# Gated cross-attention block on one core: the first LayerNorm only centres, and its deviation scales the exponential

## The reference

```python
# x: (2, 1024, 256), ctx_1024: (2, 77, 256), 8 heads of 64
x = x + tanh(g_xattn[0]) * xattn(layernorm(x), ctx_1024, Wq, Wk, Wv, Wo, bo)
x = x + tanh(g_ffn[0]) * ffn(layernorm(x), w1, b1, w2, b2)
# layernorm: (x - mean) / sqrt(var + 1e-5)
# xattn: softmax((x Wq)(ctx Wk)^T / 8) (ctx Wv) per head, then @ Wo + bo
# ffn: linear 256 -> 1024, relu, linear 1024 -> 256; inputs, hidden values
#      and weights rounded to fixed point of 8 bits
```

## Time and profile before

| | |
|---|---|
| median of 3 runs (lowest to highest) | 129.49 us (129.15 to 129.62) |
| the profiled execution | 129.84 us, of which the span of its instructions is 127.9 us |
| busy share PE, PEld, DVE, ACT, POOL | 95%, 86%, 78%, 56%, 73% |
| chain that ended last, by engine | PE 55%, POOL 27%, issue 7%, DVE 5% |
| starts of PE's slots 0 to 9, us | 21.86, 27.79, 33.62, 38.55, 46.95, 52.20, 57.87, 63.94, 69.97, 76.38 |

### The profile page before, as it was taken

How to read it: one execution, slowest core, us unless ns; L and a number is a source line. 1 busy time by engine, 2 the same in 40 slices (tenths; PEclk the granted TensorE clock), 3 DMA queues, 4 the chain that set the end, 5 groups by cost and what they waited for, 6 DMA issues and landing times.

```text
span 127.9 us, 2834 instructions
## 1 busy us (share of the span) xinstructions
PE 121.3 (95%) x996; PEld 110.4 (86%) x996; DVE 99.8 (78%) x221; ACT 71.3 (56%) x151; POOL 93.7 (73%) x175
## 2 busy tenths in 40 slices
PE   7999999999995999999999999999999999999990
PEld 2698978989893799999999899999999999888780
DVE  6109888599999879999897969697887979547882
ACT  4124625599793828499392829282837546365520
POOL 3002873777979898989998998988768596987720
PEclk9999999999999999999999999999999999999999
DMA  3898898100000000000002000200020020001014
GB/s 113 244 297 300 292 399 350 68 3 5 3 3 0 0 0 8 0 0 0 5 0 82 0 0 5 82 0 3 5 82 0 0 85 5 0 29 58 24 58 164
DMA packets 5572, 8.86 MB, mean 69 GB/s; under 512 B 1180, under 2 KB 2743, under 8 KB 5431
## 3 DMA queue, kind: packets, MB, share of 16 engines
q1 hardware_dynamic: 5559, 8.69, 19.2%
HBM read 6.59 MB, written 2.10 MB: 68 GB/s over the span
## 4 chain that ended last, share of the span: by engine, by line
PE 55%; POOL 27%; issue 7%; DVE 5%; DMA 2%; ACT 2%; POOLq 0%; DVEq 0%
PE of_ps L776 12%; PE sc_ps L743 11%; PE h_ps L803 7%; PE of_ps L818 6%; PE tr_ps L692 5%; PE tr_ps L755 4%; POOL rstd L286 4%; POOL yq L290 4%; POOL x_sb L343 3%; POOL probs L277 3%; POOL hid L322 3%; POOL xn L272 3%; DMA ctx_sb<-in_ctx_dram 2%; POOL rstd L266 2%; PE h_ps L712 1%
## 5 line engine op out<-in xcount | busy, mean ns | idle before, releaser
L776 PE MATMUL of_ps<-u_sb,pT 128*128 128x256 f32 x240 | 31.5, 282 | 0.3
L743 PE MATMUL sc_ps<-a_sb,xT 128*128 128x308 f32 x192 | 31.2, 311 | 0.0
L776 PEld LDWEIGHTS of_ps<-u_sb,pT 128*128 128x128 f32 x240 | 29.9, 188 | 1.0 <-issue 0.7
L743 PEld LDWEIGHTS sc_ps<-a_sb,xT 128*128 128x128 f32 x192 | 27.5, 189 | 0.8 <-issue 0.6
L422 ACT ACTIVATE hid_q<-h_ps,b1z 128x256 int8<-128x256 f32 x58 | 24.9, 495 | 3.9 <-PE h_ps L803 3.9
L396 ACT ACTIVATE probs<-probs 128x616 f32<-128x616 f32 x16 | 11.6, 722 | 27.7 <-DVE probs L547 27.7
L277 POOL TENSOR_TENSOR probs<-probs,rden 128x616 f32<-128x616 f32 x16 | 19.6, 1224 | 3.7 <-DVE rden L557 3.7
L542 DVE TENSOR_REDUCE mx<-sc_ps 128x8 f32<-128x616 f32 x16 | 12.7, 792 | 7.4 <-PE sc_ps L743 7.4
L322 POOL CAST hid<-hid_q 128x512 bf16<-128x512 int8 x27 | 15.9, 613 | 2.0 <-ACT hid_q L422 2.0
L803 PE MATMUL h_ps<-x2T,w1T 128*128 128x256 bf16 x128 | 16.6, 273 | 0.0
L408 ACT CAST pT<-tr_ps 128x640 fp32r<-128x640 f32 x16 | 11.0, 690 | 7.1 <-PE tr_ps L755 6.8
(11 more groups left out here) (105 smaller groups left out, 184.7 us busy)
## 6 DMA issues: line engine op xcount, KB each, us to landing
w_sb<-in_L_ffn_w_dram SPq DMA_DIRECT2D x2, 1024.0 KB, 11.3
out_dram<-x_sb SPq DMA_DIRECT2D x7, 256.0 KB, 2.5
x_sb<-in_x_dram SPq DMA_DIRECT2D x4, 256.0 KB, 8.2
x_sb<-in_x_dram SPq DMA_DIRECT2D x1, 1024.0 KB, 11.5
wk_sb<-in_L_xattn_Wk_dram SPq DMA_DIRECT2D x2, 256.0 KB, 3.7
wq_sb<-in_L_xattn_Wq_dram SPq DMA_DIRECT2D x1, 512.0 KB, 5.9
wv_sb<-in_L_xattn_Wv_dram SPq DMA_DIRECT2D x1, 512.0 KB, 7.7
wo_sb<-in_L_xattn_Wo_dram SPq DMA_DIRECT2D x1, 512.0 KB, 7.7
```

Of the source, the lines that this page charges most:

```text
L743: ins = nc.tensor.matmul(sc_ps[:, a, 0:HALF], xT[:, T % 2, p, c, :], a_sb[:, q, T // TB, c, HALF * a:HALF * a + HALF], start=first, stop=last)
L776: ins = nc.tensor.matmul(attn_ps, pT[:, T % 2, p, P * c:P * c + P], u_sb[:, q, MC * (T // TB) + c, :], start=first, stop=last)
```

## The change

The rows that go into the scores are now only centred, and with the sign turned: xn = mean - x. The sign and the softmax's 1/8 go into A (`wqT` is copied with the scale -1/8), and the missing division by the deviation becomes the scale of the exponential, one number per row (`rstd1`). The centring of tiles 2 to 15 is an activation on ScalarE (`minus_centred`, L378 after), that of tiles 0 and 1 is on VectorE (L627 after). GpSimd keeps only the reciprocal deviation, always for two tiles. VectorE's statistics come as one tile a slot in slots 1 to 10. In the prologue the context comes as two loads, one from ScalarE, and there is one more warm-up matmul; TensorE's transposes of tiles 0 and 1 stand ahead of the values' projection and the first scores between its two halves; the copy of `vz` for the second pair moves from VectorE to ScalarE.

```diff
-WARM = 6
+WARM = 7
-FIRST_OF = (0, 2, 4, 6, 8, 12)
+FIRST_OF = tuple(range(0, TILES, 2))
...
         def _(sp):
-            sp.dma_start(ctx_sb[:, :, :], ctx_in.rearrange("b m d -> m b d")).then_inc(ctx_in_sb, 16)
+            sp.dma_start(ctx_sb[:, 0, :], ctx_in[0, :, :]).then_inc(ctx_in_sb, 16)
...
-                nc.gpsimd.tensor_scalar(nm1[:, t], mv1[:, t, 0], -1.0, 1.0, ALU.mult, ALU.mult).then_inc(ve1_ready, 1)
-            def normalise_first(T):
-                pool.wait_ge(rstd1_ready, T + 1)
-                if T >= 2:
-                    pool.wait_ge(xT_psum, T - 1)
-                nc.gpsimd.tensor_scalar(xn[:, T % 2, :], x_sb[:, T, :], nm1[:, T:T + 1], rstd1[:, T:T + 1],
-                                        ALU.add, ALU.mult).then_inc(xn_ready, 1)
...
             for s in range(TILES):
-                if s == 2:
-                    rstd_first(6, 8)
-                if s == 4:
-                    rstd_first(8, 12)
-                if live(s + 4) and s > 0:
-                    normalise_first(s + 4)
                 if live(s - 1):
                     normalise_second(s - 1)
                 if live(s + 1):
                     softmax_scale(s + 1)
                 if s in (0, 1):
                     a_low(s, s + 1)
+                if s % 2 == 1 and 3 <= s < TILES - 4:
+                    rstd_first(s + 3, s + 5)
...
-                if s == 6:
-                    rstd_first(12, 16)
...
+            def minus_centred(T):
+                act.wait_ge(mv1_ready, T + 1)
+                act.wait_ge(xT_psum, T - 1)
+                nc.scalar.activation(xn[:, T % 2, :], x_sb[:, T, :], ACT.Identity, bias=mv1[:, T, 0:1],
+                                     scale=-1.0).then_inc(xn_ready, 1)
+
             def exponentials(T):
+                act.wait_ge(rstd1_ready, T + 1)
                 act.wait_ge(centered, T + 1)
-                nc.scalar.activation(probs_v(T), probs_v(T), ACT.Exp, scale=SCALE).then_inc(exp_done, 1)
+                nc.scalar.activation(probs_v(T), probs_v(T), ACT.Exp, scale=rstd1[:, T:T + 1]).then_inc(exp_done, 1)
...
+            act.dma_start(ctx_sb[:, 1, :], ctx_in[1, :, :]).then_inc(ctx_in_sb, 16)
             act.wait_ge(ctxT_psum, 1)
...
-                nc.scalar.copy(wqT[:, 2 * j:2 * j + 2, :].rearrange("p c n -> p (c n)"), h_ps[:, j, :]).then_inc(wqT_ready, 1)
+                nc.scalar.activation(wqT[:, 2 * j:2 * j + 2, :].rearrange("p c n -> p (c n)"), h_ps[:, j, :], ACT.Copy,
+                                     scale=-SCALE).then_inc(wqT_ready, 1)
...
                 if live(s + 3):
                     xT_copy(s + 3)
+                if live(s + 4) and s > 0:
+                    minus_centred(s + 4)
...
             stats_first(0, 2)
-            stats_first(2, 4)
+            for T in range(2):
+                dve.wait_ge(mv1_ready, T + 1)
+                nc.vector.tensor_scalar(xn[:, T, :], x_sb[:, T, :], mv1[:, T, 0:1], -1.0, ALU.subtract,
+                                        ALU.mult).then_inc(xn_first, 1)
...
-                if 1 <= s <= 5:
-                    stats_first(4 + 2 * s, 6 + 2 * s)
+                if 1 <= s and live(s + 5):
+                    stats_first(s + 5, s + 6)
                 if live(s + 2):
                     center(s + 2)
...
-            pe.wait_ge(ctx_in_sb, 16)
+            pe.wait_ge(ctx_in_sb, 32)
```

More of the change, by code:

```diff
@@ L263, in rstd_first @@
                 nc.gpsimd.tensor_scalar(ve1[:, t], mv1[:, t, 1], EPS, 1.0, ALU.add, ALU.mult).then_inc(ve1_ready, 1)
-                nc.gpsimd.tensor_scalar(nm1[:, t], mv1[:, t, 0], -1.0, 1.0, ALU.mult, ALU.mult).then_inc(ve1_ready, 1)
-                pool.wait_ge(ve1_ready, 2 * len([T for T in FIRST_OF if T <= first]))
+                pool.wait_ge(ve1_ready, len([T for T in FIRST_OF if T <= first]))
                 nc.gpsimd.tensor_tensor(rstd1[:, t], ve1[:, t], mhalf[:, 0:end - first], ALU.pow).then_inc(rstd1_ready, end - first)
-            def normalise_first(T):
-                pool.wait_ge(rstd1_ready, T + 1)
-                if T >= 2:
-                    pool.wait_ge(xT_psum, T - 1)
-                nc.gpsimd.tensor_scalar(xn[:, T % 2, :], x_sb[:, T, :], nm1[:, T:T + 1], rstd1[:, T:T + 1],
-                                        ALU.add, ALU.mult).then_inc(xn_ready, 1)
             def softmax_scale(T):
@@ L468, in _ @@
                 nc.scalar.copy(head_blocks(vz, 0, q), pair_bank(0, q)).then_inc(v01_ready, 1)
+            minus_centred(2)
+            minus_centred(3)
+            act.wait_ge(v_psum, 2)
+            for q in range(2):
+                nc.scalar.copy(head_blocks(vz, 1, q), pair_bank(0, q)).then_inc(v23_ready, 1)
             xT_copy(2)
+            exponentials(0)
             u_copy(0, 0)
-            exponentials(0)
             u_copy(0, 1)
             u_copy(0, 2)
+            minus_centred(4)
             act.wait_ge(g_in, 32)
@@ L635, in _ @@
                                     ALU.subtract).then_inc(xT_ready, 2)
-            dve.wait_ge(v_psum, 2)
-            dve.wait_ge(vz_zero, 1)
-            for q in range(2):
-                nc.vector.tensor_copy(head_blocks(vz, 1, q), pair_bank(1, q)).then_inc(v23_ready, 1)
+            stats_first(2, 4)
             center(0)
+            stats_first(4, 6)
             rowsT_low(2)
+            denominators(0)
             u_low(0, 0)
-            denominators(0)
             u_low(0, 1)
@@ L710, in output_weights @@
                     c, row = g // (P // WIN), WIN * (g % (P // WIN))
+                    if (b, j, col) == (0, 2, 0):
+                        pe.wait_ge(v23_ready, 2)
                     dst = u_banks[b, c // 2][:, D * (c % 2):D * (c % 2) + D]
@@ L737, in scores @@
                 for p, q in PARTS:
+                    if q == 1 and T == 0:
+                        pe.wait_ge(a_ready, 2)
                     if p == 1:
@@ L861, in _ @@
             pe.wait_ge(ctxT_ready, 1)
-            keysT(wk_sb, k_psum, (0, 1))
+            keysT(wk_sb, k_psum, (0, 1), 0)
             pe.wait_ge(wk_in[1], 16)
-            keysT(wk_sb, k_psum, (2, 3))
+            keysT(wk_sb, k_psum, (2, 3), 1)
             pe.wait_ge(wq_in, 16)
@@ L882, in _ @@
                 ins.then_inc(xT_psum, 1)
-            keysT(wv_sb, v_psum, (2, 3))
-            pe.wait_ge(a_ready, 2)
+            pe.wait_ge(wv_in, 16)
+            keysT(wv_sb, v_psum, (0, 1), 0)
+            pe.wait_ge(a_high, 2)
+            pe.wait_ge(a_ready, 1)
             scores(0)
-            pe.wait_ge(v23_ready, 2)
+            pe.wait_ge(v01_ready, 2)
+            keysT(wv_sb, v_psum, (2, 3), 0)
             rowsT(2)
             pe.wait_ge(wo_in, 16)
-            pe.wait_ge(v01_ready, 2)
             output_weights(0)
```

19 lines of the change are left out of this document (5 added, 14 removed).

## The result

| | before | after |
|---|---|---|
| median (lowest to highest), 4 runs each | 129.40 us (129.15 to 129.62) | 125.75 us (125.38 to 126.05) |
| the profiled execution, its span | 129.84, 127.9 us | 126.05, 124.1 us |
| starts of PE's slots 0 to 5, us | 21.86, 27.79, 33.62, 38.55, 46.95, 52.20 | 20.40, 26.41, 32.21, 36.99, 43.81, 49.13 |
| starts of slots 6 to 9 and 12, us | 57.87, 63.94, 69.97, 76.38, 94.54 | 54.75, 60.75, 66.75, 72.75, 90.75 |

The ratio is 0.9715, with an interval of 0.9685 to 0.9744: 2.85% faster. The two rows of slot starts show where.

A forecast was written before the change was run, and what follows sets the result against it. PE bounds the kernel, so only its waits can be regained: 1.59 and 0.32 (GpSimd), 0.33 (VectorE), 2 times 0.06 (cold starts), less 0.05, make 2.3 us. Forecast 127.2 us, own range 126.6 to 127.9, 8 in 10 125.3 to 128.4.

The forecast's parts named there:

- GpSimd's removed work: Slots 3 and 8: with normalisations, pair and mean gone, PE's waits of 1.59 and 0.32 us for GpSimd go.
- VectorE's statistics: Slots 1 and 2: one tile a slot brings the residual earlier and ends PE's wait, 0.33 us (0.25 to 0.50).
- ScalarE's new work: Centring on ScalarE, some 0.5 us a slot, is hidden and costs nothing; without cover in slot 1, 0.5 us once.
- The prologue: Before slot 0: PE has next to no gap, so moving blocks gains nothing; 0.05 us taken as loss.
- TensorE's clock rises earlier: Rival, chance 0.17: longer warm-up raises the clock during the keys; Wq 1.2 us sooner, transposes up to 0.4; 125.6 us.
- Two context loads: Prologue: splitting the context's load saves only issue time and brings it no sooner; costed at nothing, -0.1 to +0.3 us.
- 129.9 us for a context 3 us late: Rival, chance 0.05: the context's second load, started by ScalarE, lands late and delays all that follows on PE.
- The 0.05 for the seventh matmul: Prologue: the seventh warm-up fills PE's 0.22 us wait and may move the context's transposes by 0.0 to 0.2 us.
- Cold starts: Blocks after a wait on PE start cold, 0.77 us in place of 0.71; 2 times 0.06 us gained.
- The sum behind slot 0: GpSimd's 1.59 and 0.32, VectorE's 0.33 and 2 times 0.06 for cold starts; 2.36 us without the prologue's 0.05.

The follow-up runs named there:

- the control: The changed kernel itself, run again without an edit in the set of the halved Wq load: 125.82 us (125.31 to 126.08, 6 runs), ratio 0.9730.

## Why the prediction was right, and where it failed

**GpSimd's removed work: right in sum.** Slot 3 gained 1.58 us and slot 8 0.41; the forecast had 1.65 and 0.38. No wait of PE for GpSimd is left. The margin in slot 3 is 0.33 us, forecast 0.19. Not all of it is GpSimd's, though: with the statistics in pairs slot 3 keeps 1.32 (8.40 to 7.08). And the reason was put too broadly. The prediction counts "16 normalisations of 558 ns" among what goes; eleven of them put back at 480 ns bring back 0.21 us of waiting and 0.1 us in all. Most of the 2.07 us was the pair and the mean in front of the second LayerNorm, and by elimination that is what counted. (By the prediction's own numbers PE arrives at 38.44 and not 38.42, so its margin was 0.21.)

**VectorE's statistics: the mechanism was right, the term mis-sized.** It said 0.33 us (0.25 to 0.50), all of it one wait for the residual; undoing the part costs 0.80. The 0.33 counts one wait of PE. VectorE has hardly a gap in slots 1 to 5, so a pair of tiles is late for more than the residual: in slots 3 and 5 PE loses at the attention's output too. Those 0.27 and 0.11 us were not looked for. VectorE at 5.51 us of 6.00 in slots 6 to 10 (forecast 5.6) did no harm.

**ScalarE's new work: right.** A centring takes 525 ns (forecast 500) and is hidden. Slot 1 has ScalarE at 5.31 of 5.80 us. The exponential never waits for `rstd`. What wasn't in the forecast: its scale per row costs 95 ns an instruction, hidden too, by these groups of the changed kernel (count | busy us, mean ns | idle before):

```profile
L384 ACT ACTIVATE probs<-probs,rstd 128x616 f32<-128x616 f32 x16 | 13.1, 817 | 23.0 <-DVE probs L545 23.0
...
L378 ACT ACTIVATE xn<-x_sb,mv 128x256 f32<-128x256 f32 x14 | 7.2, 525 | 0.5 <-DVE mv L535 0.5
```

**The prologue: this step failed.** It said that "moving its blocks gains nothing" and put the whole at -0.05 us; it was 1.46, so the time is outside the forecast's own range of 126.6 to 127.9 us. The sentence reads one profile, in which PE had no gap between the keys and slot 0, and takes the instant at which the clock rises as given. At a given instant the moved blocks do gain nothing: from the block behind the Wq transposes to slot 0 it takes 10.93 us, and took 10.87. The step that failed is the clock, left at its late instant in the sum. Two things were missed.

First, that instant is not fixed by the program. It can be read where the starts of the single matmuls come closer, to about 0.1 us:

| PE's pause ahead of the context's transposes | the clock rises at, us |
|---|---|
| none over 0.05 us (11 profiles) | 3.5, 3.9, 5.1, 5.5, 5.6, 5.8, 5.8, 6.4, 6.5, 6.7, 6.8 |
| 1.90 us (two warm-ups) | 7.3 |
| 0.20 us (two context loads in the kernel before) | 9.2 |
| 0.22 us (before) | 10.2 |

The 6.7 of after and the 3.9 of the control are the same program. The Trainium skill (TensorE: Matmul & The Clock Gate, What's actually happening) says that the instant differs from run to run, and puts it at 0.5 us to either side. The control bears the first out and differs by more, 2.8 us. Every profile with a pause has a later instant than every one without, though the longest pause has not the latest. So the pause that the seventh matmul fills very likely matters. It doesn't act alone: six warm-ups leave no pause when the context lands by 3.5 us, and then the clock rises early too.

Second, an early clock is worth little in the kernel before, which gives back 1.1 us of it in waits (13.38 against 12.28 us), 0.9 of that at the scores, where VectorE's statistics of tiles 2 and 3 hold up `a_sb`. The changed kernel keeps nearly all of it. Of what the change does there, the prediction looked at TensorE's order and not at the call taken out of VectorE's. By the timelines that call is the larger part; TensorE's moved blocks have no price that a run shows, since the run that moves one makes a third order.

So the rival "TensorE's clock rises earlier" (chance 0.17, 125.6 us) is what came, together with the forecast's 2.3 us, and 125.75 us lies in the wider range, 125.3 to 128.4, because of that rival. Its price was right in both parts, 1.2 and 0.4 us for 1.16 and 0.36. That the changed prologue would keep this gain, where the old one doesn't, it didn't ask: there it was lucky. The argument against it, that the runs of before lie close together, was weak: the rise at 6.4 in place of 10.2 us moves slot 0 of the kernel before by only 0.57 us, so close times don't show a steady instant. What fixes the instant stays open.

**Two context loads: right** by the medians, 129.13 us against 129.19. (The prediction's 129.9 us for a context 3 us late should be 130.2, its 127.2 and 3; nothing hangs on it.) The 0.05 for the seventh matmul was nothing: the context's transposes start at 3.70 us in both profiles. **Cold starts**: the transposes of slot 3 take 0.71 us now, and the 0.06 is inside slot 3's 1.58. **The sum behind slot 0** came out at 2.33 us for 2.3 with the help of a term it doesn't have: the layout gives 0.34. That part of the match is luck. The terms that it has gave about 2.0. Slot 2 gained 0.15 of its 0.33, and slots 0 and 4 lost 0.08 and 0.07.

Not tried: the kernel before with the whole new prologue and nothing else, which would give the 1.1 us alone; the same with only `stats_first(2, 4)` moved; and the changed kernel with TensorE's old order in full. These three would share the 1.1 us out.

## What to carry to other kernels

An order without gaps in one profile says only that it fits that execution's clock; where TensorE's rise differs between executions, cost each order at an early and at a late instant, and look on the other engines for an instruction that waits for a load ahead of what TensorE wants. Keep a block of other work between transposes and the matmuls that read them: without one TensorE waited 0.82 us. Where two engines are both without slack, their terms trade: undo one alone before believing either's size. On GpSimd look at the form of an instruction as well as its size before moving it away.

## What the runs showed of the hardware

- One program's TensorE took the 16 key matmuls in 2.34 and in 3.18 us in two executions; of the other twelve profiles ten have 2.34 to 3.44 us and two 4.36 and 4.44. The clock rose at 3.5 to 6.8 us in the 11 without a pause ahead of the context's transposes and at 7.3 to 10.2 in the 3 with one.
- After a wait of 1.57 us and 1.7 us of work at the full rate TensorE ran at half rate from 10.3 to nearly 14 us in one execution; after a wait of 1.20 us in another it did not.
- GpSimd's operation on 128 x 256 with two operations takes 1145 ns as subtract then multiply by a constant, 480 ns as multiply by a constant then add, and 558 ns as add then multiply with two row operands. VectorE does subtract and multiply in 340 ns.
- A scale that is read per row makes ScalarE's exponential of 128 x 616 take 817 ns, not 722. The Trainium skill (ScalarE: Activation LUTs, What ACT_TABLE_LOAD costs) gives about 93 ns for each such operand, and the 95 agree.
- 64 bytes of another table's allocation change 15 matmuls of 128x256, start to next block, from 1.71 to 1.77 and 1.79 us in slots 5 to 11; in slots 2 and 3 they take 1.80 without it.
